# The first expert's tokens of a mixture-of-experts block turned by TensorE instead of by DMA, and their gather indexed straight from the table

## The reference

```python
logits = x @ gate_weight.T
probs = softmax(logits)
topw, topi = top_k(probs, 8)                       # 8 of 32 experts for each of the 4096 tokens
topw = topw / topw.sum(-1, keepdims=True)
pos = (cumsum(oh) * oh).sum(-1) - 1                # a token's place in its expert's list
buf = zeros((32, 512, 512)).at[flat_e, pos].set(flat_x, mode='drop')
gate, up = split(einsum('ech,efh->ecf', buf, gate_up_proj))
eo = einsum('ecf,ehf->ech', silu(gate) * up, down_proj)
out = sum over the 8 of (topw * eo[flat_e, pos])
x = layernorm(x + out)
```

## Time and profile before

| | us |
|---|---|
| median of 3 runs | 1942.58 (1940.3 to 1944.5) |
| the profiled execution, its own time | 1942.89 |
| its span, first to last instruction | 1941.1 |
| TensorE busy | 1822.3 (94% of the span) |
| VectorE, ScalarE, GpSimd busy | 1159.2, 976.0, 1216.8 |
| mean granted TensorE clock | 0.971 of full |
| attention and routing end (last `fill_slots` matmul) | 1119.6 |
| expert 0's first matmul | 1137.5 |
| expert 1's first matmul | 1163.3 |

### The profile page before, as it was taken

One profiled execution on the slowest core, in us unless ns is written; L12 is line 12 of the kernel. 1 busy time (PEld: TensorE's weight loads), 2 busy tenths in 40 slices (PEclk: granted clock), 3 DMA queues, 4 the chain that ended last, 5 costly groups with the idle time before them and its releaser, 6 DMA issues.

```text
span 1941.1 us, 43227 instructions
## 1 busy us (share of the span) xinstructions
PE 1822.3 (94%) x15526; PEld 1081.9 (56%) x15526; DVE 1159.2 (60%) x2139; ACT 976.0 (50%) x1967; POOL 1216.8 (63%) x993
## 2 busy tenths in 40 slices
PE   7999999999999999999996679999999999999980
PEld 4776677677767777677763334444444444444430
DVE  5556778777877787778776634444444444444434
ACT  6766676566657665766563213333333333333314
POOL 3766776777677767776774036666666656566631
PEclk9999999999999999999998789999999999999995
DMA  8766676666565766576557389999999999999949
GB/s 240 143 130 122 131 145 135 130 130 154 131 132 120 157 138 134 109 157 146 135 98 166 114 213 234 238 234 242 235 235 243 243 246 248 234 238 235 199 58 351
DMA packets 621486, 345.69 MB, mean 178 GB/s; under 512 B 521456, under 2 KB 543984, under 8 KB 621424
## 3 DMA queue, kind: packets, MB, share of 16 engines
q1 hardware_dynamic: 592480, 274.62, 58.9%
q0 software_dynamic: 28944, 70.27, 17.4%
HBM read 158.67 MB, written 60.29 MB: 113 GB/s over the span
## 4 chain that ended last, share of the span: by engine, by line
PE 88%; issue 3%; ACT 3%; DVE 3%; DMA 2%; POOL 1%; SPq 0%; ACTq 0%; DVEq 0%; POOLq 0%
PE bank L657 62%; PE bank L1096 12%; PE bank L723 5%; PE bank L695 5%; PE bank L834 1%; ACT arena_wo L1508 1%; PE bank L667 1%; PE bank L756 1%; PE bank L841 0%; PE bank L791 0%; DMA stage<-arena_r 0%; DVE s_max L1548 0%; ACT qk L1153 0%; DMA stage<-wkT 0%; DMA acc_rows<-arena_wo,cur_to 0%
## 5 line engine op out<-in xcount | busy, mean ns | idle before, releaser
L657 PE MATMUL bank<-arena_x,arena_wo 128*128 128x256 f16 (+1 forms) x4224 | 609.7, 302 | 8.6 <-ACT qk L1153 5.3
L657 PEld LDWEIGHTS bank<-arena_x,arena_wo 128*128 128x128 f16 x4224 | 407.8, 98 | 196.9 <-issue 11.2
L2334 POOL DMA_INDIRECT acc_rows<-arena_wo,cur_to x128 | 274.4, 2144 | 241.0 <-ACT arena_wo L1493 211.6
L2116 POOL TENSOR_TENSOR arena_p<-arena_p 128x512 f16<-128x512 f32 x256 | 330.1, 1311 | 110.9 <-ACT arena_p L1172 110.8
L1518 DVE SCALAR_TENSOR_TENSOR arena_wo<-stage,arena_wo 128x3072 f16<-128x3072 f32 (+2 forms) x72 | 179.4, 2493 | 288.9 <-ACT arena_wo L1240 280.8
L657 PE MATMUL bank<-arena_v,arena_wo 128*128 128x512 f16 x1152 | 253.7, 382 | 12.6 <-issue 12.6
L1096 PE MATMUL bank<-arena_wo 128*128 128x512 f16 x1116 | 245.9, 379 | 0.0
L2111 POOL TENSOR_TENSOR qk<-qk 128x512 f16<-128x512 f32 x128 | 160.6, 1255 | 114.8 <-ACT qk L1153 114.8
L1163 ACT ACTIVATE arena_p<-bank,s_neg 128x256 f32<-128x256 f32 x512 | 203.0, 503 | 15.8 <-DVE s_neg L1551 13.5
L1493 ACT ACTIVATE arena_wo<-bank,cur_w 128x512 f32<-128x512 f32 x128 | 79.8, 685 | 256.8 <-PE bank L1096 246.9
L1151 ACT ACTIVATE qk<-bank,bqkv 128x256 f32<-128x256 f32 x256 | 122.9, 480 | 152.3 <-PE bank L657 151.8
(11 more groups left out here) (161 smaller groups left out, 2297.2 us busy)
## 6 DMA issues: line engine op xcount, KB each, us to landing
stage<-wguT SPq DMA_DIRECT2D x32, 1536.0 KB, 9.4
stage<-wdnT SPq DMA_DIRECT2D x32, 768.0 KB, 12.3
arena_x<-xT SPq DMA_DIRECT2D x16, 512.0 KB, 4.2
arena_r<-x_rows SPq DMA_DIRECT2D x16, 512.0 KB, 5.1
stage<-ctxT SPq DMA_DIRECT2D x16, 512.0 KB, 4.4
x_rows<-arena_r SPq DMA_DIRECT2D x16, 512.0 KB, 3.1
acc_rows<-arena_r SPq DMA_DIRECT2D x16, 512.0 KB, 3.3
arena_wo<-acc_rows SPq DMA_DIRECT2D x8, 1024.0 KB, 10.9
```

Of the source, the lines that this page charges most:

```text
L657: mm = pe.matmul(out_ap, lhs(a, i), rhs(c, i), start=(n == 0 and i == 0), stop=(n == 2 and i == chunks - 1))
L2116: gp.tensor_tensor(halves[:, j % 2, h, 1, :], probs[:, j % 2, h].rearrange("p t k -> p (t k)"), halves[:, j % 2, h, 0, :], ALU.subtract).t ...
L2334: gp.indirect_dma_start(acc_rows, bass.IndirectOffsetOnAxis(ap=cur_to[:, k, c:c + 1], axis=0), y[:, k, c, :], None, compute_op=ALU.add).th ...
```

## The change

Expert 0's four chunks are no longer turned by SP's DMA transposes. TensorE turns each chunk by eight transposes (a matmul of the 128x128 float16 block with an identity `ident16`) into one PSUM bank of float16, and ScalarE (chunks 0 and 2) or VectorE (chunks 1 and 3) copies the bank to `xgT[0]`. `first_mm` counts turned chunks, `first_turned` copied ones; TensorE's expert 0 and GpSimd's gather of expert 1 wait for four of the latter. `gather_first` no longer copies the index column, and its DMAs read their indices from `idx_from`. The counts of `xg_turned[0]` and `from_done` go down by one expert everywhere.

```diff
+        ident16 = sb("ident16", [P, P], F16)
+        ps_first = [b[:, :].bitcast(F16).rearrange("p (m n) -> p m n", m=2 * DC) for b in bank[4:8]]
+        first_mm, first_turned = sem("first_mm"), sem("first_turned")
-        N_CONST, N_CONSTV = 12, 7
+        N_CONST, N_CONSTV = 12, 8
...
-            def turn_first():
-                for c in range(CC):
-                    sp.wait_ge(ld_first[c], 16)
-                    sp.dma_start_transpose(xgT[0][:, :, c * P:(c + 1) * P], xg_parts[:, 0, c, :]).then_inc(xg_turned[0], 16)
-
             sp.wait_ge(slot_mm, B)
-            turn_first()
             load_expert(2, 1)
             turn_tokens(1, 1, 64)
...
-            expert(0, 0, 64)
+            def turn_first(c):
+                pe.wait_ge(ld_first[c], 16)
+                for m in range(2 * DC):
+                    mm = pe.transpose(ps_first[c][:, m, :], xg_parts[:, 0, c, m * P:(m + 1) * P], ident16[:, :])
+                mm.then_inc(first_mm, 1)
+
+            pe.wait_ge(s_constv, N_CONSTV)
+            for c in range(CC):
+                turn_first(c)
+            pe.wait_ge(first_turned, CC)
+            up_gate(0, 0, 0)
+            down(0, 0)
...
+            def first_out(c):
+                act.wait_ge(first_mm, c + 1)
+                nc.scalar.activation(xgT[0][:, :, c * P:(c + 1) * P], ps_first[c], ACT.Copy).then_inc(first_turned, 1)
+
+            first_out(0)
+            first_out(2)
...
+            vec.tensor_copy(ident16[:, :], ident[:, :]).then_inc(s_constv, 1)
...
+            def first_out(c):
+                dve.wait_ge(first_mm, c + 1)
+                vec.tensor_copy(xgT[0][:, :, c * P:(c + 1) * P], ps_first[c]).then_inc(first_turned, 1)
...
                 gate_up_lo(1, 1, 0)
+                first_out(1)
+                first_out(3)
                 down_lo(1, 1, 0)
...
             def gather_first():
-                column(cur_from, 0, idx_from, 0, from_done)
-                wait_apart(pool, from_done, 1, s_const, N_CONST)
                 for c in range(CC):
                     gp.indirect_dma_start(xg[:, 0, c, :], None, x2_rows,
-                                          bass.IndirectOffsetOnAxis(ap=cur_from[:, 0, c:c + 1], axis=0)).then_inc(ld_first[c], 16)
+                                          bass.IndirectOffsetOnAxis(ap=idx_from[:, 0, c:c + 1], axis=0)).then_inc(ld_first[c], 16)
...
-            pool.wait_ge(xg_turned[0], 64)
+            pool.wait_ge(first_turned, CC)
             gather(1, 1)
```

More of the change, by code:

```diff
@@ L1078, in up_gate @@
             def up_gate(e, k, turned):
-                pe.wait_ge(xg_turned[k], turned)
+                past(pe, xg_turned[k], turned)
                 pe.wait_ge(ew_lo_gu, count(e, 1, 1))
@@ L1116, in _ @@
             pe.wait_ge(warm, WARM_START + sum(WARM_ROUTE) + WARM[0] + WARM[1] + WARM_FIRST)
-            expert(0, 0, 64)
+            def turn_first(c):
[9 more added lines that the diff above has]
+            down(0, 0)
             expert(1, 1, 64)
             with pe.Fori(1, NX // 2 - 1) as m:
-                expert(m * 2, 0, count(m, 64, 64))
+                expert(m * 2, 0, count(m, 64))
                 expert(m * 2 + 1, 1, count(m, 64, 64))
-            expert(NX - 2, 0, NX // 2 * 64)
+            expert(NX - 2, 0, (NX // 2 - 1) * 64)
             up_gate(NX - 1, 1, NX // 2 * 64)
@@ L2318, in gather @@
                 column(cur_from, k, idx_from, e, from_done)
-                wait_apart(pool, from_done, count(e, 1, 1), s_const, N_CONST)
+                wait_apart(pool, from_done, count(e, 1), s_const, N_CONST)
                 for c in range(CC):
@@ L2338, in expert @@
                 pool.wait_ge(s_const, N_CONST)
-                pool.wait_ge(xg_turned[k], turned)
+                past(pool, xg_turned[k], turned)
                 weights_out(e, k)
@@ L2357, in _ @@
             pool.wait_ge(table, 2 * TABLE)
-            pool.wait_ge(xg_turned[0], 64)
+            pool.wait_ge(first_turned, CC)
             gather(1, 1)
-            expert(0, 0, True, True, 64)
+            expert(0, 0, True, True, 0)
             expert(1, 1, True, True, 64)
             with pool.Fori(1, NX // 2 - 1) as m:
-                expert(m * 2, 0, True, True, count(m, 64, 64))
+                expert(m * 2, 0, True, True, count(m, 64))
                 expert(m * 2 + 1, 1, True, True, count(m, 64, 64))
-            expert(NX - 2, 0, True, False, NX // 2 * 64)
+            expert(NX - 2, 0, True, False, (NX // 2 - 1) * 64)
             expert(NX - 1, 1, False, False, NX // 2 * 64)
```

## The result

| | before | after |
|---|---|---|
| median of 12 runs each, us | 1942.17 (1940.06 to 1944.5) | 1946.8 (1940.15 to 1958.6) |
| the profiled execution, its own time | 1942.89 | 1945.67 |
| its span | 1941.1 | 1943.9 |
| expert 0's first matmul | 1137.53 | 1135.27 |
| TensorE's waits for tokens behind it | none | 3.4 and 0.4 |

What follows compares the result with a forecast made beforehand. TensorE bounds the kernel, idle 12.62 us before expert 0 (the hole). Landing 1132.95 + transposes 1.0 + copy 1.2 + hand-overs 0.15 = 1135.3 instead of 1137.53: 2.2 us less, median 1940.4, range 1937.2 to 1943.9.

Steps and rivals of the forecast that it cites:

- Index column: Ahead of expert 0's first gather: dropping the column copy gains 0.25 or 1.09 us there, nothing at the fourth.
- D: Rival, chance 0.07: expert 0's third gather starts before VectorE's split and escapes its hold; 3.5 us gained in all, 1939.1.
- Fourth gather: Expert 0's last gather on GpSimd: 0.95 us instead of 1.36, landed at 1132.95, 1.35 us earlier.
- Eight transposes: TensorE turning expert 0's last chunk at half clock: 1.0 us, from seven steps and one full latency of 0.28.
- B: Rival, chance 0.08: transposes don't overlap, each takes some 0.28 us; eight are 2.2 us, gain 1.0, 1941.6.
- Copy out of PSUM: VectorE's 128x1024 copy of the last chunk before expert 0: 1.2 us, from the price of PSUM reads.
- Loads of expert 2 moved up: SP's weight loads go from 1135.59 to about 1119.7, beside expert 0's gathers: nothing on the path, the least certain zero.
- C: Rival, chance 0.09: expert 2's loads collide with expert 0's gathers; expert 0 starts at 1140.05, 2.5 us slower, 1945.1.
- Clock: Expert 0 on TensorE: 5.0 us at 0.50 and then 1.00, the same ramp from the new start.
- A: Rival, chance 0.10: the clock stays up through TensorE's transposes and expert 0; 5.1 us gained in all, 1937.5.
- Behind the hole: After expert 0's start: expert 1's gathers move along with TensorE's start, and TensorE still never waits; no cost.
- E: Rival, chance 0.06: expert 1's tokens come late and TensorE waits there instead, so nothing is gained; 1942.6.

Runs made afterwards that it cites:

- the exchange: Changed kernel with expert 2's four transposes issued on SP ahead of expert 3's two loads: 1939.4 us, ratio 0.9988.

## Why the prediction was wrong

The median was forecast at 1940.4, and it is 1946.8. The hole closed, and more than it gave was lost behind it.

**The hole, link by link: right in the mechanism.** Expert 0's start was forecast at 1135.3 and is 1135.27. That the two agree so closely is luck. Counted from the end of `idx_to`, the hole took 12.44 us where 13.24 was forecast, 0.8 less, and this execution came out of routing 0.77 later.

- *Index column.* Forecast: worth 0.25 or 1.09 us at the first gather, nothing at the fourth. Measured 0.87 at the first; nothing at the fourth, since VectorE's split holds the third. Right, and so is D's refusal: nothing escaped in any of the traces looked at.
- *Fourth gather.* Forecast 0.95 us on GpSimd, landed 3.75 after its start. Measured 0.95 and about 3.5 (1129.92 to 1133.45).
- *Eight transposes.* Forecast 1.0, measured 1.04 at a granted clock of 0.50. No row of before showed the 0.28 us of latency in this term (its four float32 transposes are 0.15 each); measured are 0.13 for each transpose in a row. B, that each takes its latency, is out.
- *Copy out of PSUM.* Forecast 1.2, measured 0.69. I carried the price of float32 reads over to float16. The estimate of 0.65 worked out from the Trainium skill (VectorE: DVE Perf Modes, § The perf-mode tier table) was the better one, and the trace agrees with its up to 2x. The 0.5 us won here is part of the 0.8.
- *Loads of expert 2 moved up.* Forecast nothing on the path; measured nothing. C is out: the fourth gather landed by 1133.45, where it needed 1135.15.
- *Clock.* Forecast: the same ramp from the new start. Half clock at the start was right, but it lasted less: 0.63 on the mean from 1134 to 1140, and 17.27 us for the 72 matmuls in place of 18.13, another 0.86 us gained. A is out for this execution, but see below.

**The step that failed is "Behind the hole".** It said that expert 1's gathers move "along with TensorE's start" and that TensorE "still never waited", and E was set aside because the tokens "depend on the same event as TensorE's start". That is true of GpSimd and false of SP. Three things were missing. The first and the last could be read from the trace of before; of the second only that the neighbours would change:

1. I followed expert 1 only. Expert 1 was never late, in any trace. The queue behind it is in order, and it was the tokens of experts 2, 3 and 4 that came late.
2. I asked how much earlier each thing starts, not what it then lies beside. Expert 1's transposes move 2.65 us forward and take 11.77 us in place of 6.92, so SP comes out of them 2.2 us *later* while expert 1 on TensorE and the scatters are 3.1 us *earlier*. The two sides of the race moved apart by 5.3 us.
3. The row of 14.47 us, where the other experts' groups take 5.4 to 9.6, stood in SP's timeline before. It marks the one group that has a load directly ahead of it. That was the weak place, hidden by 15.5 us between its end (1171.11) and TensorE's start of expert 2 (1186.58). The change left 7.9 of them, and moved the first scatter from 6.4 us into the group to 1.1.

E was right in kind and wrong in place and size: it let TensorE wait where it had gained, so that the most it could lose was the gain. A queue that runs late loses more than that, 5.4 us in one trace and 18 in another. No rival of mine had a loss from behind the hole. The term "Behind the hole" stood at nothing in the sum; 5.4 us of loss belong there in the profiled execution.

**With SP's order the other way round the forecast's number comes out**: with the exchange the time is 2.9 us below the kernel before on the same chip (1942.3 - 1939.4), where 2.2 was forecast; 0.7 us of difference is within what runs scatter (the interval is 0.6 to 4.1 us).

What stays open. Why expert 1's transposes, with no load near, take 9.8 to 12.8 us in the seven traces of the changed kernel and its variants in which expert 2's gathers are not held (they start 1.3 to 2.9 us ahead of them), and 5.4 to 6.6 in the four traces in which these are held, although expert 2's, forced beside expert 3's gathers, took only 7.65. In the five other traces of the kernel before and its variants, where expert 2's gathers aren't held either, it is 6.2 to 7.0. In the run with the exchange, expert 3's and 4's took 12.6 and 11.4, also with the load over 11 us away, and expert 4's gathers behind the former. So the load is shown for expert 2's group alone, and the gathers may have a part of some 5 us that comes and goes. Then, how the load slows the transposes: the DMA engines' busy share over expert 2's group is 1.12 with 239 GB/s moved in after, and 1.09 with 174 GB/s in the run with the exchange, where the group takes 6.21 us, so the share doesn't tell them apart. And the high runs of which no trace was taken: one at 1954.99 with the index column alone, three at 1949.67 to 1955.51 with expert 2's load ahead of expert 0's transposes, one at 1950.15 with expert 3's gathers held. The first four are of kernels in which TensorE starts no more than 0.7 us earlier, so an early TensorE may not be needed for a high run.

## What to carry to other kernels

When a change lets the critical engine start earlier, list the transfers that other queues have in flight for the next stages, with what each lies beside before and after, and look first at a group in the timeline that is already much longer than its sisters: here that was the place where it broke. An in-order queue can run later although every event that it waits for comes earlier. Here the small transfers that were due soon belonged ahead of a large load that wasn't, and a single exchange in that order can be worth nothing before a change and more than the whole of the change after it. When the runs of a kernel fall into groups, one profile is one draw: count the high runs of each variant, for that count told more here than the medians.

## What was not expected of the hardware

**Transposes raised the clock.** In the trace with expert 2's gathers held, TensorE's transposes for expert 0, and the stretches around them (length, busy and instructions of PE, PEld, DVE, ACT, POOL, then granted clock, DMA share, GB/s):

```profile
1128.29 3.05 PE L1117 MATMUL bank<-ident,arena_p 128*128 128x128 f16 x24 [4.28 <-DMA arena_p<-x_rows,idx_from]
1131.79 0.62 PE L1117 MATMUL bank<-ident,arena_p 128*128 128x128 f16 x8 [0.45 <-DMA arena_p<-x_rows,idx_from]
1133.20 15.71 PE L654 MATMUL bank<-arena_v,arena_wo 128*128 128x512 f16 x72 [0.79 <-DVE arena_v L1795]
```

```profile
1128.00:1130.00 2.00, 1.57 (x14) 1.34 (x15) 0.00 (x0) 0.66 (x1) 1.14 (x2) 0.51 0.54 156
1130.00:1132.00 2.00, 1.55 (x17) 1.19 (x15) 0.69 (x1) 0.98 (x2) 0.00 (x0) 0.64 0.48 137
1132.00:1134.00 2.00, 1.21 (x12) 0.64 (x10) 1.55 (x2) 1.69 (x2) 0.73 (x1) 1.00 0.00 0
```

Since the end of the keep-warm matmuls, TensorE had done nothing but 24 float16 transposes when the clock went from 0.50 (1.2 GHz) to 1.00 (2.4 GHz); the last eight took 0.62 us in place of 1.04, and expert 0 ran at 15.71 us in place of 17.27. The trace with expert 3's gathers held shows the same (0.58 from 1130 to 1132, then 1.00), and these two have the shortest spans of all profiled runs, 1934.2 and 1934.4 us. In after, with as many transposes, it stayed at 0.50 until expert 0. So A can happen, in some executions; what decides it is open. The Trainium skill (TensorE: Matmul & The Clock Gate, § Part 4: PE-mode transpose) says that the full clock doesn't engage for transposes. The trace doesn't agree: by that the last eight would have taken 1.04 us, and they took 0.62.

**An indirect DMA waits for a table only 0.29 us** when it reads its indices where VectorE left them, and 1.16 when GpSimd copies the column first, of which the copy itself is 0.18. And GpSimd's copy of 4 elements in each partition beside VectorE's split took 1.58 us instead of 0.19 (1135.35 above). It ends 0.05 us behind the split, as the third gather ends 0.83 behind the one it falls into.
